# Two edits in the attention stage of a decoder layer: the gate's two small products in another shape, and an earlier start of the output projection

## The reference, cut to what matters

```python
q = rotate(silu((x @ Wq).reshape(b, n, 16, 32)));  k = rotate(silu((x @ Wk).reshape(...)));  v = x @ Wv
o = lightning_attn(q, k, v, log_lam)        # chunks of 128 tokens, a state carried from chunk to chunk
gate = x @ Wg1 @ Wg2                        # 512 -> 32 -> 512: a product of rank 32
xg = o * sigmoid(gate)
xg = xg * rsqrt(mean(xg * xg over each head's 32) + 1e-6)
x = layernorm(x + (xg * norm_weight) @ Wo)
```

## Time and profile before

| | |
|---|---|
| median of 3 runs | 967.49 us (965.09 to 968.42) |
| the profiled execution | 969.0 us |
| its span | 967.2 us |
| TensorE busy, whole span | 833.6 us (86%) |
| VectorE, ScalarE, GpSimd busy | 642.9, 399.9 and 478.4 us |
| share of the chain that ended last | PE 71%, DVE 11%, issue 8%, DMA 3%, ACT 3%, POOL 2% |
| granted TensorE clock, mean | 0.936 |
| stages | attention until the first transpose of the next stage (L787) at 353.4 us; token-id experts and routing; routed experts from 548.0 us (L898) to 909.5 us (last L909); last sums and norm |

### The profile page before, as it was taken

One profiled execution on the slowest core, in us unless ns is written; L12 is line 12 of the kernel. 1 busy time (PEld: TensorE's weight loads), 2 busy tenths in 40 slices (PEclk: granted clock), 3 DMA queues, 4 the chain that ended last, 5 costly groups with the idle time before them and its releaser, 6 DMA issues.

```text
span 967.2 us, 18058 instructions
## 1 busy us (share of the span) xinstructions
PE 833.6 (86%) x5736; PEld 709.9 (73%) x5737; DVE 642.9 (66%) x1454; ACT 399.9 (41%) x805; POOL 478.4 (49%) x443
## 2 busy tenths in 40 slices
PE   6899999999999749999995299999999999999710
PEld 5787888778877538888884198888888888888600
DVE  6767656775677536777777667676676767766526
ACT  5332323222322412233322046666666666566504
POOL 0332342233333422555555357777777677767434
PEclk9999999999999669999998589999999999999955
DMA  9631121112111031332222369999999999999687
GB/s 330 219 133 45 45 87 43 43 43 78 52 43 34 23 111 49 104 104 94 94 92 94 94 179 275 266 261 278 272 267 261 279 278 257 263 272 277 142 253 291
DMA packets 72540, 155.37 MB, mean 161 GB/s; under 512 B 9952, under 2 KB 10384, under 8 KB 72112
## 3 DMA queue, kind: packets, MB, share of 16 engines
q1 hardware_dynamic: 49920, 99.40, 31.1%
q0 software_dynamic: 22576, 55.42, 23.7%
HBM read 110.27 MB, written 44.52 MB: 160 GB/s over the span
## 4 chain that ended last, share of the span: by engine, by line
PE 71%; DVE 11%; issue 8%; DMA 3%; ACT 3%; POOL 2%; DVEq 0%; SPq 0%; POOLq 0%; ACTq 0%
PE ps L575 25%; PE ps L909 18%; PE ps L922 11%; PE ps L898 3%; PE ps L669 2%; DVE arena L1309 2%; PE ps L612 1%; PE ps L678 1%; PE ps L819 1%; PE ps L603 1%; PE ps L621 1%; PE ps L723 1%; PE ps L741 1%; DVE arena L1690 1%; POOL arena L1758 1%
## 5 line engine op out<-in xcount | busy, mean ns | idle before, releaser
L909 PE MATMUL ps<-arena,raw 128*128 128x192 f32 x1152 | 200.0, 331 | 9.4 <-DVE arena L1629 9.0
L909 PEld LDWEIGHTS ps<-arena,raw 128*128 128x128 f32 x1152 | 189.4, 192 | 20.2 <-issue 10.0
L1849 POOL DMA_INDIRECT y_rows<-arena,place_token x96 | 153.8, 1602 | 90.1 <-issue 71.3
L1840 POOL DMA_INDIRECT w_lo<-x_rows,place_token x96 | 106.9, 1114 | 43.1 <-issue 28.3
L575 PE MATMUL ps<-w_hi,x_hi 128*128 128x512 f32 (+1 forms) x332 | 78.5, 359 | 4.4 <-DVE x_lo L1364 3.7
L1658 DVE TENSOR_TENSOR w_hi<-raw,w_hi 128x512 fp32r<-128x512 f32 x48 | 33.2, 692 | 63.8 <-ACT w_hi L1131 51.3
L575 PE MATMUL ps<-w_lo,x_hi 128*128 128x512 f32 (+1 forms) x332 | 74.4, 347 | 0.0
L1114 ACT ACTIVATE arena<-ps,arena 96x512 f32<-96x512 f32 x48 | 32.8, 683 | 100.2 <-PE ps L922 98.6
L575 PE MATMUL ps<-w_hi,x_lo 128*128 128x512 f32 (+1 forms) x332 | 74.1, 346 | 0.0
L1712 POOL TENSOR_TENSOR arena<-arena,attn_pack 128x512 f32<-128x512 f32 x12 | 16.8, 1403 | 114.4 <-DVE arena L1255 114.4
L922 PE MATMUL ps<-w_hi,x_hi 128*96 128x512 f32 x192 | 63.4, 412 | 10.0 <-DVE o_hi L1663 4.9
(11 more groups left out here) (218 smaller groups left out, 1817.7 us busy)
## 6 DMA issues: line engine op xcount, KB each, us to landing
raw<-in_gu SPq DMA_DIRECT2D x48, 768.0 KB
raw<-in_dn SPq DMA_DIRECT2D x48, 256.0 KB
raw<-in_dn SPq DMA_DIRECT2D x48, 128.0 KB
y_rows<-zero SPq DMA_DIRECT2D x20, 256.0 KB
arena<-in_xT SPq DMA_DIRECT2D x16, 256.0 KB, 3.2
x_res<-in_x SPq DMA_DIRECT2D x16, 256.0 KB, 2.7
raw<-in_ctxw SPq DMA_DIRECT2D x1, 4096.0 KB, 14.8
x_rows<-x1o SPq DMA_DIRECT2D x16, 256.0 KB, 2.0
```

The source lines that it names most:

```text
L909: m = pe.matmul(out, wgu[p][:, q, part * P:(part + 1) * P], xgT[:, p, q, :], start=(q == 0), stop=(q == KC - 1))
L1840: pool.indirect_dma_start(out=xg[:, place, h, :], out_offset=None, in_=x2_d, in_offset=bass.IndirectOffsetOnAxis(ap=place_token[:, 2 * n + ...
L1849: pool.indirect_dma_start(out=(y_d, y2_d)[p], out_offset=bass.IndirectOffsetOnAxis(ap=place_token[:, 2 * n + h:2 * n + h + 1].bitcast(U32) ...
```

## The change

- The first product (`gate_low`) no longer adds up over k. Each of its four matmuls has Wg1 once (32 columns) and writes its own 32 partitions, so that the four go to four column tiles of the array, and the result is four partial sums on 128 partitions.
- ScalarE copies these 128 rows in plain fp32 to `g1`. VectorE's `low_g1` is gone, and so are the splitting of Wg2 at the start (one ScalarE and one VectorE instruction) and the three semaphores.
- The second product (`gate_high`) goes over 128 rows: Wg2 stands four times on the partitions, and the partial sums are added up by it. Its operands are fp32 in place of fp32r. It waits for ScalarE's copy alone.
- Wg2 is loaded four times in place of three, and the packed constants hold Wg1 once in place of three times.
- `project_o` waits for `o_high` at its start and for `oT_copied` only ahead of its third pass.
- On VectorE, `low_o` moves from in front of the cut of the state's part (L1340) to behind it, in front of the state's sum.

```diff
-             ("dq", P, (G, P)), ("block", P, (P,)), ("wg1", P, (KC, 3 * RANK))]
+             ("dq", P, (G, P)), ("block", P, (P,)), ("wg1", P, (KC, RANK))]
...
-        wg2 = take("wg2", [3 * RANK, D]); wg2_parts = sb("wg2_parts", [3 * RANK, D], F32R)
-        g1_parts = sb("g1_parts", [3 * RANK, P], F32R)
+        wg2 = sb("wg2", [KC * RANK, D])
+        g1 = take("g1", [KC * RANK, P])
...
-            for i in range(3):
+            for i in range(KC):
                 sp.dma_start(wg2[i * RANK:(i + 1) * RANK, :], d["wg2"]).then_inc(late_in, 16)
...
-            sp.wait_ge(late_in, 80)
+            sp.wait_ge(late_in, 16 * (KC + 2))
...
                 for k in range(KC):
-                    m = pe.matmul(ps[0:3 * RANK, PM, 0:P], wg1[:, k, :], xT[:, c % 2, k, :], start=(k == 0), stop=(k == KC - 1))
+                    m = pe.matmul(ps[k * RANK:(k + 1) * RANK, PM, 0:P], wg1[:, k, :], xT[:, c % 2, k, :], start=True, stop=True, skip_group_check=True)
                 m.then_inc(g1_made, 1)
...
             def project_o(b, c, now, cuts, between=None):
                 t = 4 * b + c
-                pe.wait_ge(oT_copied, t + 1)
+                pe.wait_ge(o_high, t + 1)
...
-                three_passes(ps[:, PM, :], o_hi, o_lo, w_hi[:, 3], w_lo[:, 3], between=between).then_inc(wo_made, 1)
+                three_passes(ps[:, PM, :], o_hi, o_lo, w_hi[:, 3], w_lo[:, 3], (oT_copied, t + 1), between).then_inc(wo_made, 1)
...
             def gate_high(t):
-                pe.wait_ge(g1_low, t + 1)
+                pe.wait_ge(g1_copied, t + 1)
                 for g in range(G):
-                    m = pe.matmul(ps[:, PM, g * P:(g + 1) * P], wg2_parts[:, g * P:(g + 1) * P], g1_parts[:, :], start=True, stop=True)
+                    m = pe.matmul(ps[:, PM, g * P:(g + 1) * P], wg2[:, g * P:(g + 1) * P], g1[:, :], start=True, stop=True)
                 m.then_inc(gate_made, 1)
...
-                act.activation(g1_parts[:, :], ps[0:3 * RANK, PM, 0:P], ACT.Copy).then_inc(g1_copied, 1)
+                act.activation(g1[:, :], ps[:, PM, 0:P], ACT.Copy).then_inc(g1_copied, 1)
...
-            act.wait_ge(late_in, 80)
-            act.activation(wg2_parts[:, :], wg2[:, :], ACT.Copy).then_inc(wg2_high, 1)
...
-            def low_g1(b, c):
-                t = 4 * b + c
-                dve.wait_ge(g1_copied, t + 1)
-                part = slice(2 * RANK, 3 * RANK)
-                dve.tensor_tensor(g1_parts[part, :], ps[part, PM, 0:P], g1_parts[part, :].bitcast(F32), ALU.subtract).then_inc(g1_low, 1)
...
-                low_g1(b, c)
...
                 mask(t)
-                if not first:
-                    low_o(*last_of(b, c))
                 if c < CH - 1:
...
                     dve.tensor_tensor(whole(state_add), ps[:, PM, :].rearrange("p (g t) -> p g t", g=G),
                                       block_diag[:, :].unsqueeze(1).to_broadcast([P, G, P]), ALU.mult).then_inc(add_cut, 1)
+                if not first:
+                    low_o(*last_of(b, c))
+                if c < CH - 1:
                     dve.wait_ge(add_cut, n + 1)
...
-            dve.wait_ge(wg2_high, 1)
-            mid = slice(RANK, 2 * RANK)
-            dve.tensor_tensor(wg2_parts[mid, :], wg2[mid, :], wg2_parts[mid, :].bitcast(F32), ALU.subtract).then_inc(wg2_split, 1)
```

More of the change, by code:

```diff
@@ L344, in build @@
         ms_plus = sem("ms_plus"); rms_made = sem("rms_made"); o_normed = sem("o_normed")
-        r_spread = sem("r_spread"); r_turned = sem("r_turned"); wg2_high = sem("wg2_high"); wg2_split = sem("wg2_split"); g1_low = sem("g1_low"); oT_copied = sem("oT_copied"); wo_made = sem("wo_made")
+        r_spread = sem("r_spread"); r_turned = sem("r_turned"); oT_copied = sem("oT_copied"); wo_made = sem("wo_made")
         r1_made = sem("r1_made"); stat_made = sem("stat_made"); mv_made = sem("mv_made")
@@ L694, in a_tile @@
                 if first:
-                    pe.wait_ge(wg2_split, 1)
+                    pe.wait_ge(late_in, 16 * (KC + 2))
                 gate_high(t)
@@ L1392, in _ @@
             rotated_sum(0, 0, 1)
-            dve.wait_ge(wg2_high, 1)
-            mid = slice(RANK, 2 * RANK)
-            dve.tensor_tensor(wg2_parts[mid, :], wg2[mid, :], wg2_parts[mid, :].bitcast(F32), ALU.subtract).then_inc(wg2_split, 1)
-            dve.wait_ge(late_in, 80)
+            dve.wait_ge(late_in, 16 * (KC + 2))
             tiles_of_a(dve, a_tile, CH - 1)
@@ L1907 @@
         "wo": rows(a["L0_attn_Wo"]),
-        "wg1": np.tile(rows(a["L0_attn_Wg1"]), (1, 1, 3)),
+        "wg1": rows(a["L0_attn_Wg1"]),
         "wg2": a["L0_attn_Wg2"],
```

## The result

The changed kernel takes 961.98 us (median of 20 runs, 959.52 to 966.47), the kernel before on the same chip 967.34 (20 runs, 964.59 to 970.47 but for one of 2898.11, which stands far apart). The ratio is 0.9954 with an interval of 0.9940 to 0.9967. That is 5.4 us by the medians and 4.5 by the ratio. The forecast was 962.1.

The account below looks back on a forecast made before the run. A loop through all engines, not TensorE, bounds the attention. Savings 0.28 + 0.33 + 0.85 + 0.84 + 1.62 + 0.60 + 0.20 + 0.73 = 5.45 us take 969.0 to 963.6; forecast median 962.1, range 958 to 966.6.

Parts of the forecast that it names:

- TensorE isn't the bound; a loop through all engines is: Attention's steady passes: TensorE, busy 288.16 of 303 us, stands at two or three places where a loop through all engines closes.
- First product 0.51: `gate_low` in four column tiles: two steps, 0.21, plus 0.30 for switching in and out; 0.51 us instead of 0.85.
- Second product 0.85: `gate_high` in fp32: eight instructions instead of four, 0.85 us, adding 0.46; bounds 0.42 and 1.8.
- It stays covered: Ahead of `turn_r`: 0.12 us more TensorE work lies within slack of 0.30, 0.30, 0.43 and 0.21, so costs nothing.
- the gate outgrows its cover: Rival, chance 0.08: column tiles run one after the other, 0.76 us more per pass against 0.30 slack; 968.5 us.
- The projection's start: Output projection starts earlier: 0.30 us in c = 0, 0.60 in c = 1, c = 2 alike, 0.54 in c = 3.
- VectorE's bubble: Gap on VectorE between L1340 and L1346, filled by `low_o`: 0.22 us in c = 1, 0.11 in c = 0.
- Only half of it arrives: Rival, chance 0.19: the gap behind the cut isn't filled, since the state's sum still waits for its semaphore; 3.6 us, 963.9.
- The start: Tile 0: without `low_g1` and the Wg2 split VectorE is over 1 us earlier, and the mask starts 0.28 earlier.
- Tile 15 and the last projection: Attention's end: tile 15's gate without `low_g1` wins 0.2 us (0 to 0.3); the last projection starts 0.73 earlier.
- tile 13's 0.60: Tile 13's projection in the pass of tile 14: no further v projection follows, so its whole 0.60 us is won.
- clock rival: Attention's end: half-clock stretches move by a third to either side, 3 to 5 us; 958 or 966.5, chance 0.06 each.

Follow-up runs that it names:

- the gate's run: The changed kernel with the output projection's edits undone, so the gate's edits alone: 961.17 us, ratio 0.9989 to the kernel before.
- the first four experiments: On chip 5: gate's edits alone 961.17 us; projection's waits alone 958.84; waits and order, old gate 957.62; changed kernel with `low_x` and epsilon earlier 957.84.

## Why the prediction was right, step by step

**TensorE isn't the bound; a loop through all engines is.** Shown. TensorE's busy time in the stretch is unchanged, the time falls by 3.92. With 0.90 added, TensorE does become the bound (9.72 in every pass from the v projection to the scores).

**First product 0.51.** Mis-sized, in the good direction: the block takes 0.36, and the block ahead of it grows by 0.07 (0.81 to 0.88), 0.43 in all. Two steps of 0.107 and 0.15 for leaving are 0.36, as the rows of L678 gave; entering costs 0.07, not 0.15. The four tiles do run beside each other. The price of the mode switch that the Trainium skill warns of ("TensorEngine Tiling (Array Packing)", Key Properties) is 0.22 here. The tiles save 0.53 (0.89 - 0.36) with the exit counted and 0.46 with the entry too.

**Second product 0.85.** Right within 0.04: 0.89 from its start to the next block's where TensorE sets the time. For the old one, 4 x 0.11 = 0.44 is an estimate from its instructions' starts, which are 0.11 apart; no run shows it with TensorE as the limit. With it TensorE has about 0.03 more, and with the 0.40 that I had taken 0.07, not 0.12.

**It stays covered.** Right in its result, and shown twice (230.18 in the gate's run with c = 0 and 3 unchanged; 223.49 against 223.56). The cover itself was read too generously: I took the gap ahead of `turn_r` as slack, while the floor measured by doubling the product leaves 0.12 to 0.29. The margin to the rival "the gate outgrows its cover" was thin. Without the column tiles it is through, and costs 0.29 in c = 0 and 3.

**The projection's start.** Right in place and size. In c = 3 the 0.54 came as 0.62, and the waits alone bring it. In c = 0, 1 and 2 the waits alone bring nothing, since the projection still waits for the cut. With the cut ahead of `low_o` it starts earlier by 0.3 (without the delay) to 0.65 (with it, in c = 1 and 2), and the low part of x takes back all but VectorE's bubble, as argued. That bubble was predicted at 0.11, 0.22 (and 0.26 at the v projection) and 0.28, and measured at 0.11, 0.25 and 0.27 by adding the order, or 0.13, 0.26 and 0.30 in the two profiles. "Only half of it arrives" is thereby out. A forecast of 3.45 us for the three rounds of passes stands against 3.92 and 3.74.

**The start.** The 0.28 for tile 0 is real, but another wait took its place where it was measured. On chip 5 the two kernels with the old gate have tile 0's mask 1.59 behind the scores, those with the new one 1.24 and 1.25: 0.35 won. In the changed kernel's own profile it is 1.62, as late as before (1.58 in the earlier trace rows), though VectorE has stood for 2.04 us:

```profile
29.10 1.17 PE L669 MATMUL ps<-arena 32*128 32x128 f32 x32
30.14 1.20 POOL L1720 DMA_INDIRECT token_of_slot<-name_of,name_to  x1 [0.94 <-POOL name_of L1717]
30.72 2.48 DVE L1301 TENSOR_TENSOR arena<-ps,arena 128x512 f32<-128x512 f32 x4 [2.04 <-PE ps L669]
```

VectorE is over 1 us earlier, as forecast, and with it the sort, and so the indirect store, which used to come at 30.73, after the mask's start, and now comes before it. With the store held back (chip 7) tile 0's mask comes 1.24 behind the scores with the new gate and 1.59 with the old one. So the step that failed is "the mask starts 0.28 earlier": I had priced the added issue on the start's queues, and not the store that an earlier sort brings ahead of the mask. At this place it is a 0.3 us term and decides nothing. The 2.63 by which tile 2 comes later fits the clock. Tile 0's scores start at 29.10 instead of 27.60 already: in the first projections four 512-wide matmuls take 1.64 to 1.71 us instead of 0.91 until 14.38 us, in the kernel before 1.71 until 10.86 and then once 1.20, and the trace's first record of the full clock is at 14.28 and 11.46 us. And tile 1 has 3.4 us more at half the clock. That the edits moved either is not shown; over all runs tile 0's scores start at 26.85 to 28.39 with the old gate and at 27.37 to 29.10 with the new one.

**Tile 15 and the last projection.** The 0.73 is shown: the projection starts 0.05 after the high part (331.58 + 0.63), not 0.78. Tile 15's 0.20 fits: from the first product to the spread of the power 5.13 us became 316.87 - 312.00 = 4.87, with GpSimd as the new end of the wait, as feared for that place. Together with tile 13's 0.60 I had 1.53 for the end, and it measured 4.22. The other 2.7 is beyond what the edits explain. In the third window the clock was granted at 0.73 before and 0.80 after; on chip 2 50.68 became 46.64 at 0.79 and 0.83. Of half-clock time in it there is 27.9 us before and 19.6 after. So my clock rival, at a chance of 0.06 to each side, was partly at work: gains in the end, losses of 2.63 at the start and 2.15 behind the attention. That the grant favours the end of the changed kernel in both pairs may be chance or not. On chip 5 the kernel with the gate's edits alone has 51.28 there, the one with the waits alone 49.75, the one with waits and order 48.3. The end thus gets shorter with the projection's edits, but the half-clock time differs too (25.0, 21.1 and 19.2 us), and nothing here tells how much of it the edits cause.

**The sum.** 5.45 was forecast. Medians give 5.4 and 6.3 (chip 2), ratios 4.5 and 4.9. The steady passes gave 0.3 to 0.5 more than forecast, the 0.28 of the start is missing in the changed kernel's profile, and the clock's share, of either sign, is as large as the rest of the error. So the mechanism and the size of the steady gain are borne out. That the median lies within 0.2 us of the forecast is partly luck: the interval of the ratio reaches from 3.2 to 5.8 us.

## What to carry to other kernels

Look for the loop across engines before counting matmuls: where TensorE's stops close a loop, a wait that is moved off the stop pays only in passes where nothing else is due right behind it, and elsewhere only the filled bubble on the engine that is late next. To size cover, double the covered work and read the floor that comes out; a gap ahead of a waiting instruction overstates it. Compare kernels by a stretch with a full clock in both, since the whole time carries the clock's scatter.

## What the runs showed of the hardware that I had not expected

- VectorE's mask can start late behind TensorE's scores beside GpSimd's indirect store. Scores to mask takes 1.24 us without it. In tiles 1 to 14 it takes 1.55 to 1.70 where the store ends 1.21 to 1.30 us after the scores' start, 1.38 to 1.46 where it ends 1.00 to 1.09 after, and 1.24 again where it ends within 0.67. On chip 5, in the first four experiments, the same overlap left 1.24. Whether the signal comes late or VectorE is held back the profile doesn't tell. What makes the chips differ is open, and tile 0 (the rows above: the store ends at 31.34, after the mask's start) doesn't fit the simple account that VectorE waits for the store's end.
- Leaving 128x32 column tiles cost 0.15 us and entering them 0.07; eight fp32 matmul instructions in four column tiles went in 0.36, where eight untiled ones, 128 columns wide, took 0.89. On this shape an fp32 matmul is two instructions, started 0.11 apart, and an fp32r one a single such instruction, so three fp32r parts in 96 rows cost about half of fp32 over 128 rows (0.44, an estimate from the starts, and 0.89).
- GpSimd's power of 128x16 took 2.90 to 2.95 us alone and 3.01 to 3.04 where a 0.55 us VectorE instruction started some 0.3 us ahead of it. It took 4.77 or 4.78 in tile 15 of every run, beside a 2.28 us one (L1367; L1375 in the kernel before).
- The stretches at half the clock move from execution to execution of nearly the same program: in tile 1 there were 0, 3.4 or 6.8 us of it, and the scores of tile 2 started anywhere from 66.89 to 71.67.
